# Attention steps without MLP: twelve score tiles one step ahead in place of eight, with new instruction orders on four engines

## The reference

```python
h = softmax((q @ k.T) * scale) @ v        # 16 heads, 256 x 256 scores each
x = x + gate * (h @ Wo + bo)
x = x + gate2 * (gelu(norm(x) @ W1 + b1) @ W2 + b2)   # layers 0, 1, 3 only
```

## Time and profile before

| what | us |
|---|---|
| median of 3 runs | 1170.08 |
| span of the profiled execution | 1170.3 |
| TensorE busy | 1081.3 |
| VectorE busy | 746.0 |
| ScalarE busy | 569.9 |
| GpSimd busy | 174.5 |

### The profile page before, as it was taken

The page is one execution under the profiler, slowest core; times in us unless marked ns, Lnnn a source line. Parts: engine busy times, 40 slices in busy tenths (PEclk is TensorE's granted clock), DMA queues, the critical chain, the costliest instruction groups (busy, mean ns, idle before and its releaser), DMA issues.

```text
span 1170.3 us, 21598 instructions
## 1 busy us (share of the span) xinstructions
PE 1081.3 (92%) x7618; PEld 858.1 (73%) x7618; DVE 746.0 (64%) x2091; ACT 569.9 (49%) x1140; POOL 174.5 (15%) x288
## 2 busy tenths in 40 slices
PE   5899999999999999999999988888888999999997
PEld 4568878788787787888787755556556877887776
DVE  4476656766567666667665666666667666676632
ACT  4254565554553445544446434444445556555452
POOL 3011110111113111101111101111114111011110
PEclk9799999999999999999999999988999999999999
DMA  7732333222345223331233433323343133321300
GB/s 236 244 115 63 102 110 109 80 65 73 110 155 186 77 78 110 110 110 60 69 102 109 137 111 102 115 94 109 110 152 128 58 100 119 119 89 66 106 4 19
DMA packets 102715, 123.21 MB, mean 105 GB/s; under 512 B 8992, under 2 KB 96032, under 8 KB 101600
## 3 DMA queue, kind: packets, MB, share of 16 engines
q1 hardware_dynamic: 102048, 121.73, 33.4%
q10 hardware_dynamic: 576, 0.30, 0.1%
HBM read 85.16 MB, written 35.78 MB: 103 GB/s over the span
## 4 chain that ended last, share of the span: by engine, by line
PE 71%; DVE 10%; DMA 8%; ACT 5%; issue 3%; SPq 1%; ACTq 1%; POOL 0%; DVEq 0%; POOLq 0%
PE dense L1179 13%; PE o_banks L1256 9%; PE dense L1110 9%; PE dense L1165 9%; PE s_bank L1203 8%; DMA q_stack<-max_t 7%; PE st_bank L1240 6%; PE o_banks L1139 4%; DVE neg_max L805 3%; PE o_banks L1264 3%; PE o_banks L1089 2%; ACT probs L613 2%; PE o_banks L1125 2%; PE s_bank L1213 2%; PE st_bank L1232 1%
## 5 line engine op out<-in xcount | busy, mean ns | idle before, releaser
L613 ACT ACTIVATE probs<-st_bank 128x512 f32<-128x512 f32 (+1 forms) x512 | 264.5, 570 | 172.9 <-PE st_bank L1240 121.7
L805 DVE TENSOR_REDUCE neg_max<-s_bank 128x2 f32<-128x512 f32 x384 | 256.7, 685 | 120.9 <-PE s_bank L1203 117.5
L1203 PE MATMUL s_bank<-k_stack,q_stack 96*128 96x256 f32 (+1 forms) x1024 | 233.9, 319 | 19.2 <-DMA k_stack<-qk_dram 10.1
L1203 PEld LDWEIGHTS s_bank<-k_stack,q_stack 96*128 96x128 f32 x1024 | 169.9, 194 | 61.7 <-DVE neg_max L805 20.2
L1179 PE MATMUL dense<-w_sb,hid 128*128 128x256 f32 x768 | 204.9, 381 | 0.0
L1240 PE MATMUL st_bank<-q_stack,k_stack 98*128 98x512 f32 x384 | 152.8, 471 | 15.6 <-DMA q_stack<-max_t 12.5
L444 POOL TENSOR_TENSOR veps<-mv,eps_c 128x2 f32<-128x2 f32 x65 | 13.7, 210 | 901.7 <-DVE mv L771 901.7
L1179 PEld LDWEIGHTS dense<-w_sb,hid 128*128 128x128 f32 x768 | 128.8, 189 | 9.6 <-issue 0.4
L601 ACT ACTIVATE hid<-dense,vec 128x256 f32<-128x256 f32 x192 | 80.6, 471 | 110.8 <-PE dense L1165 110.7
L1256 PE MATMUL o_banks<-probs,v_aug 128*32 128x256 f32 (+1 forms) x2048 | 124.9, 387 | 9.9 <-DVE xg L844 5.8
L1110 PE MATMUL dense<-ht,w_sb 128*128 128x256 f32 x512 | 127.2, 388 | 3.9 <-ACT ht L555 1.3
(11 more groups left out here) (126 smaller groups left out, 1447.5 us busy)
## 6 DMA issues: line engine op xcount, KB each, us to landing
q_stack<-qk_dram SPq DMA_DIRECT2D x192, 128.0 KB, 2.9
k_stack<-qk_dram SPq DMA_DIRECT2D x96, 256.0 KB, 4.0
par_sb<-par_dram SPq DMA_DIRECT2D x32, 512.0 KB, 5.2
qk_dram<-q_hi SPq DMA_DIRECT2D x32, 256.0 KB, 2.1
qk_dram<-q_lo SPq DMA_DIRECT2D x32, 256.0 KB, 2.2
qk_dram<-k_hi SPq DMA_DIRECT2D x32, 256.0 KB, 2.1
qk_dram<-k_lo SPq DMA_DIRECT2D x32, 256.0 KB, 2.1
w_sb<-w SPq DMA_DIRECT2D x3, 1280.0 KB, 7.5
```

What stands on the lines that cost most here:

```text
L613: nc.scalar.activation(probs[p % 4][:, kt, :, q0:N], src, ACT.Exp, scale=SCORE_SCALE[l]).then_inc(p_sb, 1)
L805: nc.vector.tensor_reduce(neg_max[:, qt, 2 * p:2 * p + 2], split3(bank[:]), AX.X, ALU.max, negate=True).then_inc(s_max, 1)
L1203: ins = mm(bank[:, e * N:e * N + k1], q_stack[g.par][0:KB, 2 * p + e, qt * P:(qt + 1) * P].bitcast(F32R), k_stack[g.par][0:KB, p, 0:k1].bi ...
```

## The change

Only steps 17 to 24 change, apart from who issues one pair of DMAs in step 16. They get orders of their own (`attention_step`) on ScalarE, VectorE and TensorE. In steps 18 to 24 twelve tiles, not eight, have been made in the step before. The high parts of q and k come behind the first and the second pair of exps, the low parts behind the maxima of tiles 12 to 15 and their split. The second residual of c moves from the end of VectorE's step to behind the third early maximum. `ao_transposed` of a step moves to ScalarE's next step. SyncE issues both pairs of row DMAs, on a semaphore for each half. The diff (blank lines are left out):

```diff
@@ -205,8 +205,9 @@
         q_hi_sb, q_lo_sb, k_hi_sb, k_lo_sb, v_sb = (
             sem(n) for n in ("q_hi_sb", "q_lo_sb", "k_hi_sb", "k_lo_sb", "v_sb"))
         q_spill, k_spill, stack_ld = sem("q_spill"), sem("k_spill"), sem("stack_ld")
-        s_ps, s_max, max_hi, max_lo, max_ps, max_sb, max_ld = (
-            sem(n) for n in ("s_ps", "s_max", "max_hi", "max_lo", "max_ps", "max_sb", "max_ld"))
+        s_ps, s_max, max_hi, max_lo, max_ps, max_sb = (
+            sem(n) for n in ("s_ps", "s_max", "max_hi", "max_lo", "max_ps", "max_sb"))
+        max_ld = [sem(f"max_ld{half}") for half in range(2)]
         st_ps, p_sb, o_ps, o_copy, ot_ps, rec_sb, ao_sb = (
             sem(n) for n in ("st_ps", "p_sb", "o_ps", "o_copy", "ot_ps", "rec_sb", "ao_sb"))
         aot_ps, aot_sb, proj_ps, prod1, xg1, x1_done = (
@@ -245,6 +246,10 @@
         def modulation_of(g):
             return MOD_STEP.index(g.off) + 1 if g.reg is None and g.off in MOD_STEP else None
+        def early_tiles(g):
+            return 3 * H // 4 if g.reg is None and 2 * B + 1 < g.off <= 3 * B else H // 2
         def modulations_before(g):
             return 1 + sum(m < g.off for m in MOD_STEP)
@@ -282,7 +287,7 @@
             for part in range(2):
                 dst = q_stack[g.par][KB + part:KB + part + 1, h0:h0 + H // 2, :]
                 src = max_t[half][part * H // 2:(part + 1) * H // 2, :]
-                eng.dma_start(dst, src).then_inc(max_ld, 16)
+                eng.dma_start(dst, src).then_inc(max_ld[half], 16)
         def cols_bank(l, norm):
@@ -350,6 +355,8 @@
             def step(g):
                 a, c, done = g.ahead(1), g.back(1), g.back(2)
                 mlp = c.exists and HAS_MLP[c.layer]
+                if c.exists and not mlp:
+                    max_rows(sp, g, 1)
                 if inputs_of(a):
                     spill(a)
                     if a.reg is None and a.off == 1:
@@ -358,7 +365,7 @@
                     stack(a)
                 if not mlp:
-                    wait(sp, max_ld, g.count(64, 64))
+                    wait(sp, max_ld[1], g.count(32, 32))
                 if g.reg is None:
                     wait(sp, x2_done, done.count(1, 1))
@@ -373,7 +380,7 @@
                     store(done)
                 if mlp:
                     max_rows(sp, g, 1)
-                if a.exists and HAS_MLP[g.layer]:
+                if a.exists:
                     max_rows(sp, a, 0)
             def store(c):
@@ -613,9 +620,29 @@
                         nc.scalar.activation(probs[p % 4][:, kt, :, q0:N], src, ACT.Exp,
                                              scale=SCORE_SCALE[l]).then_inc(p_sb, 1)
+            def attention_step(g):
+                c, a = g.back(1), g.ahead(1)
+                modulate1(a)
+                if c.off > 2 * B:
+                    ao_transposed(c)
+                exps(g, 0)
+                query_hi(a)
+                exps(g, 1)
+                key_hi(a)
+                exps(g, 2, 3)
+                value_copy(a)
+                out_copy(g, 0)
+                exps(g, 4, 5, 6, 7)
+                out_copy(g, 1)
+                if g.layer > 2:
+                    ao_transposed(g)
             def step(g):
                 c, a = g.back(1), g.ahead(1)
                 inputs, mlp = inputs_of(a), c.exists and HAS_MLP[c.layer]
+                if c.exists and not mlp:
+                    attention_step(g)
+                    return
                 if inputs:
                     modulate1(a)
                 if mlp:
@@ -818,7 +845,7 @@
             def max_copy(g, half):
                 wait(dve, max_ps, g.count(2, half + 1))
-                wait(dve, max_ld, g.count(64, 32 * half + 32 - 64))
+                wait(dve, max_ld[half], g.count(32, 0))
                 nc.vector.tensor_copy(max_t[half][:], s_bank[half % 2][0:H, 0:N]).then_inc(max_sb, 1)
             def lo_part(a, which, bank, ready, hi, dst, s, spilled):
@@ -919,8 +946,43 @@
                 for j in tiles:
                     score_max(g, j)
+            def attention_step(g):
+                c, a, n = g.back(1), g.ahead(1), g.ahead(2)
+                modulated = modulation_of(g)
+                first, early = early_tiles(g), early_tiles(a)
+                maxima(g, *range(first, H))
+                max_split(g, 1)
+                max_copy(g, 1)
+                query_lo(a)
+                key_lo(a)
+                first_residual(c)
+                wait(dve, x1_done, c.count(1, 1))
+                norm_stats(x1, 1, ln2_stats)
+                wait(dve, ln2_stats, c.count(1, 1))
+                norm_mv(1, ln2_mv)
+                second_norm(c)
+                ln1_a(n)
+                wait(dve, ln1_stats, n.count(1, 1))
+                norm_mv(0, ln1_mv)
+                out_norm(g, 0)
+                ln1_c(n)
+                maxima(a, 0, 1, 2)
+                second_residual(c)
+                maxima(a, 3, 4, 5, 6, 7)
+                max_split(a, 0)
+                if modulated:
+                    modulation_cols(modulated)
+                out_norm(g, 1)
+                max_copy(a, 0)
+                maxima(a, *range(H // 2, early))
+                if modulated:
+                    modulation_rows(modulated)
             def step(g):
                 c, a, n = g.back(1), g.ahead(1), g.ahead(2)
+                if c.exists and not HAS_MLP[c.layer]:
+                    attention_step(g)
+                    return
                 inputs = inputs_of(a)
                 modulated = modulation_of(g)
                 maxima(g, 8, 9)
@@ -1222,9 +1284,9 @@
                 for p in pairs:
                     if p == 0:
-                        wait(pe, max_ld, g.count(64, 32))
+                        wait(pe, max_ld[0], g.count(32, 32))
                     if p == PAIRS // 2:
-                        wait(pe, max_ld, g.count(64, 64))
+                        wait(pe, max_ld[1], g.count(32, 32))
                     if CAUSAL[g.layer]:
                         first, second = (split3(b[:]) for b in st_bank)
@@ -1264,8 +1326,60 @@
                         ins = tr(o_bank[i][:, N + t * P:N + (t + 1) * P], o_sb[:, i, t * P:(t + 1) * P], ident[:])
                 ins.then_inc(ot_ps, 1)
+            def attention_step(g):
+                c, a, n = g.back(1), g.ahead(1), g.ahead(2)
+                modulated = modulation_of(g)
+                first, early = early_tiles(g), early_tiles(a)
+                def modulation_part(part):
+                    if modulated:
+                        modulation_cols(modulated, part=part, parts=4)
+                score(g, *range(first, H))
+                q_product(a, 0)
+                max_turn(g, 1)
+                q_product(a, 1)
+                score_t(g, 0)
+                k_product(a)
+                score_t(g, 1)
+                v_product(a, 0)
+                score_t(g, 2)
+                v_product(a, 1)
+                score_t(g, 3)
+                projection(c, 0)
+                projection(c, 1)
+                if modulated:
+                    wait(pe, q_lo_sb, a.count(1, 1))
+                modulation_part(0)
+                values(g, 0)
+                modulation_part(1)
+                score_t(g, 4)
+                out_turn(g, 0)
+                score_t(g, 5)
+                score(a, 0, 1)
+                score_t(g, 6)
+                score(a, 2)
+                modulation_part(2)
+                score_t(g, 7)
+                score(a, 3, 4)
+                modulation_part(3)
+                values(g, 1)
+                score(a, 5, 6)
+                out_turn(g, 1)
+                score(a, 7)
+                max_turn(a, 0)
+                score(a, *range(H // 2, early - 1))
+                ht1_t(n)
+                ao_turn(g)
+                score(a, *range(max(H // 2, early - 1), early))
+                if modulated:
+                    modulation_rows(modulated)
             def step(g):
                 c, a, n = g.back(1), g.ahead(1), g.ahead(2)
+                if c.exists and not HAS_MLP[c.layer]:
+                    attention_step(g)
+                    return
                 inputs = inputs_of(a)
                 modulated = modulation_of(g)
                 score(g, 8, 9)
```

## The result

The changed kernel took 1228.86 us (median of 4 runs, 1226.48 to 1231.84), the kernel before 1170.16 (median of its runs beside it): a ratio of 1.049, 95% interval 1.045 to 1.054. So it is 59 us slower. The profiled execution has a span of 1230.1 us, where the one before had 1170.3. I had forecast 1198, with a range up to 1213: the direction was right, the size half of what came.

The account below looks back on a forecast made before the run. Each step was taken as a loop of waits across engines, none full. To 1170.3 us it added 21.7 for turns 17 to 24 and step 25 (1192 at full clock) and some 6 for half clock: 1198 us, range 1180 to 1213.

Parts of the forecast that it names:

- Low k late by the order, loads late, tile 0 waiting: Full steps: low k ends at 14.3 us behind maximum 7, not 7.6; tile 0 at 24.5, not 18.9; new wait 3.3.
- The wait of ST4 gone: ST4 on TensorE no longer waits for the DMA of the maxima's rows, which removes 0.8 us a step.
- The rows of half 1 on SyncE at no cost: Two row DMA issues of 0.7 us each on SyncE, ahead of the spill of q, were to cost nothing.
- Turns 17 and 18, step 25: Turns beside the modulation: 34.1 for 33.96 and 36.2 for 32.85 us; step 25: projection waits for ScalarE's copy, +1.1 us.
- The step that failed: Clock term of the sum, steps 17 to 24: as much half clock as before, some 6 us on top of 1192.
- my price: Cost of TensorE's half clock, from one old step: 6.8 us at half speed cost 2.1 us.
- 1192: Forecast time at full clock: 21.7 us for turns 17 to 24 and step 25, added to 1170.3.
- My own upper ends: All upper bounds together (pace of the maxima, residual, clock up to 2.1 us a turn): 1219 us.
- The nearest rival: Clock falls in every turn from tile 0 to the end of values: 2.1 us on eight turns, 1209 us, 17%.
- The Trainium skill: Guide cited: a loop waiting for a DMA leaves every wait at low clock; penalty half the throttled time, giving 1219 us.
- The faster rival: Low k to tile 0: stack loads don't set the turn if low k ends by about 10.8 us; 1164 us, 7%.
- the rival of no change: Twelve early tiles only shift work, and a shorter tail takes up low k's delay: within 0.2% of before, 3%.

Follow-up runs that it names:

- e1: Changed kernel with the products, high and low parts of q and k put back ahead of tiles 12 to 15 and the first exps: 1.068 of the kernel before.
- e3: Changed kernel plus unread matmuls on TensorE: 26 ahead of early tile 0, others behind tiles 7 to 15 except 11: 1.027 of the kernel before.
- e14: Changed kernel plus unread matmuls only at the row of maxima (behind tiles 7 to 15 except 11), none in the stack wait: 1.049 of the kernel before.
- e7: Kernel before plus unread matmuls in its own waits of steps 17 to 24, else untouched: 1.000 of the kernel before.
- e5: Changed kernel plus only the 26 unread matmuls ahead of early tile 0, in the wait for the stacks: 1.040 of the kernel before.
- e8: As e1, with the two row DMAs of half 1 given back to ScalarE, behind the copy of v: 1.052 of the kernel before.
- e9: The changed kernel itself, unaltered, measured again on another chip: 1235.24 us against 1177.33 for the kernel before, 1.051.
- e4_residual_last: Changed kernel with the second residual moved from behind early maximum 2 to behind the copy of the maxima: 1.057 of the kernel before.

## Why the prediction was wrong

- **Low k late by the order, loads late, tile 0 waiting:** right, in its place and in its size at full clock (table above). Eight waits for k_stack, of 2.7 us in the mean where 3.3 was said.
- **The wait of ST4 gone:** right. The rows of half 1 on SyncE at no cost: right for the changed kernel, and it is this that made e1 the slowest.
- **Turns 17 and 18, step 25:** forecast 34.1 and 36.2, measured 39.0 and 41.5; in e3 still 39.2 and 38.7, at a clock of 0.87 and 0.96. The modulation's two turns cost some 5 us each more than my sum (5 and 2.5 in e3), and not all of it is shown to be the clock. Step 25 was to cost 1.1 us and cost 4.6.
- **The step that failed** is the last of the sum: "Of the new steps I let as much be at half clock: 22 / 6.8 x 2.1, some 6 us." The amount was wrong: there were 120 us at half clock in the turns, not 22. The price was no better known. e3 has 97 us less of it and is 26 us faster by the ratios (give or take 9), 0.27 us for each us, near my 2.1 / 6.8 = 0.31; its profiled turns are only 17 us shorter; e14 and e7 took half clock away and gained nothing that a ratio shows. What I had put at 6 us thus cost some 30 us, by e3.
- **Luck in the numbers:** at my price the 120 us are 37 us, and 1192 + 37 = 1229, the measured time. That they agree so well is luck: those 37 us hold what turns 17 and 18 and step 25 cost beyond my sum, some of it without the clock. My own upper ends added up to 1219, above the 1213 at which I closed the range; both are below what came.
- **The nearest rival** (clock low in every turn, 1209, 17%) had the mechanism, but one stretch of 6.8 us a turn, behind the stack wait. There are two, 15 us a turn (120 / 8). I had gone through the head of the step, seen tiles 8 to 15 paced by VectorE at 0.64 us each, and counted that as time on VectorE alone. It was also ten microseconds in which TensorE had 33 matmuls, where the 14 us behind them have 77, and in which VectorE too had to wait for TensorE, 0.3 to 1.4 us at a time.
- **The Trainium skill** (TensorE: Matmul & The Clock Gate, "HAM oscillation — how this bites in real kernels") was right that a loop which waits for a DMA on every turn is at the low clock behind every wait: the trace has it in each of the eight turns, with a mean of 0.77 to 0.83, though here TensorE begins at full clock and falls 0.5 to 1.5 us later. Its price, half of the throttled time ("Terms"), would make 48 us of the 97 that e3 took away; by the ratios they were worth 26.
- The faster rival and the rival of no change fall: low k ended at 17.1, not before 10.8.

## What to carry to other kernels

When a reordering puts the small operations of one kind in a row, cost the row twice: for the engine that paces it, and for TensorE, whose clock may fall while it is fed one small tile at a time, as it did in the changed kernel, e5 and e8. Count the length of each light stretch in the new order, not only the waits. And read an in-order queue as a whole: a DMA that waits in SyncE's queue for nothing important can hold the spills that set the step.

## What the runs showed of the hardware

- Added work made the kernel faster. About 50 matmuls a step whose results nobody reads took the ratio from 1.049 (1.051 in e9) down to 1.027 (e3), and the granted clock from 0.80 to 0.96.
- Two operations of the second residual on VectorE took 0.46 to 0.47 us each in every step before. In the changed kernel they start beside POOL's addition, and one took up to 1.55 us. In `e4_residual_last`, where they come 7 us or more behind it, they have their old length. (Source rows of the changed kernel, then of e4; minimum, median and maximum in ns.)

```profile
L892 DVE SCALAR_TENSOR_TENSOR x_sb<-prod,rstd,xg x16: 472/826/1547, 674.0 to 938.7; 128x256 f32<-128x256 f32 x16
...
L892 DVE SCALAR_TENSOR_TENSOR x_sb<-prod,rstd,xg x16: 462/466/468, 692.7 to 965.8; 128x256 f32<-128x256 f32 x16
```

POOL's addition starts at the same moment (756.06 against 756.07) and lasts 1.26 us:

```profile
756.06 1.26 POOL L462 TENSOR_TENSOR xg<-x_sb,par_sb 128x512 f32<-128x512 f32 x1
```

I had given the residual 0.86 us and at worst 0.4 us of waiting. It is VectorE that is held up: its operation ends 0.3 us behind the addition, and the addition takes 1.26 to 1.28 us beside it or, in e4, without it.
